# Maxima of the first six heads from a small float32 projection, batch 1's projection beside the first slots, layer change reordered

## The reference

```python
mod = jax.nn.silu(c) @ w_adaln + b_adaln
sh_msa, sc_msa, g_msa, sh_mlp, sc_mlp, g_mlp = jnp.split(mod, 6, axis=-1)
h = _modulate(_ln(x), sh_msa, sc_msa)
qkv = (h @ w_qkv + b_qkv).reshape(B, N, 3, nh, hd).transpose(2, 0, 3, 1, 4)   # 16 heads of 9
q, k, v = (qkv[0], qkv[1], qkv[2])
attn = jax.nn.softmax(jnp.einsum('bhqd,bhkd->bhqk', q, k) * hd ** (-0.5), axis=-1)
o = jnp.einsum('bhqk,bhkd->bhqd', attn, v).transpose(0, 2, 1, 3).reshape(B, N, C)
x = x + g_msa[:, None, :] * (o @ w_proj + b_proj)
xf = _modulate(_ln(x), sh_mlp, sc_mlp).reshape(-1, C)
topk_logits, topk_idx = jax.lax.top_k(xf @ w_gate, TOP_K)
gates = jax.nn.softmax(topk_logits, axis=-1)
cw = jnp.sum(jax.nn.one_hot(topk_idx, NUM_EXPERTS) * gates[..., None], axis=1)
hmid = jax.nn.gelu(jnp.einsum('tc,ech->eth', xf, w1) + b1[:, None, :], approximate=True)
eo = jnp.einsum('eth,ehc->etc', hmid, w2) + b2[:, None, :]
return x + g_mlp[:, None, :] * jnp.einsum('te,etc->tc', cw, eo).reshape(B, N, C)
# layer 1: the same attention, then x + gate * (gelu(h @ w_fc1 + b_fc1) @ w_fc2 + b_fc2)
```

## Time and profile before

| | us |
|---|---|
| median of 3 runs | 441.26 (441.07 to 442.12) |
| the profiled execution | 441.05 |
| its span, first to last instruction | 439.2 |
| PE busy | 392.8 (89%) |
| DVE busy | 299.6 (68%) |
| ACT busy | 216.9 (49%) |
| POOL busy | 83.4 (19%) |
| mean granted clock | 0.945 |

### The profile page before, as it was taken

How to read it: one execution, slowest core, us unless ns; L and a number is a source line. 1 busy time by engine, 2 the same in 40 slices (tenths; PEclk the granted TensorE clock), 3 DMA queues, 4 the chain that set the end, 5 groups by cost and what they waited for, 6 DMA issues and landing times.

```text
span 439.2 us, 5895 instructions
## 1 busy us (share of the span) xinstructions
PE 392.8 (89%) x1938; PEld 168.1 (38%) x1938; DVE 299.6 (68%) x838; ACT 216.9 (49%) x428; POOL 83.4 (19%) x137
## 2 busy tenths in 40 slices
PE   0996699989999897999999979978989999998896
PEld 0232122323334232585856625612333333322464
DVE  7755796878887934454376526798875888961643
ACT  1245015867776784504242331056764877586420
POOL 6997999200011000000000000000000110000000
PEclk9999555999999999999999999989996999999999
DMA  6065453369200000000000243000134100000001
GB/s 182 12 99 147 149 164 95 109 188 245 73 2 2 3 0 1 0 1 1 0 1 0 82 128 115 3 0 0 61 87 147 34 3 0 3 1 1 0 0 55
DMA packets 19657, 24.12 MB, mean 55 GB/s; under 512 B 5404, under 2 KB 15904, under 8 KB 19304
## 3 DMA queue, kind: packets, MB, share of 16 engines
q1 hardware_dynamic: 14360, 21.37, 16.4%
q0 software_dynamic: 3808, 1.73, 2.4%
q10 hardware_dynamic: 1460, 0.66, 0.5%
...
...
## 4 chain that ended last, share of the span: by engine, by line
PE 68%; DVE 15%; DMA 7%; ACT 4%; SPq 3%; issue 2%; DVEq 0%; ACTq 0%
PE bank L1258 13%; PE bank L1136 12%; PE bank L1273 11%; PE bank L1285 9%; PE bank L1236 8%; DVE nmax L946 8%; PE bank L1183 3%; ACT prob L1086 2%; PE bank L1303 2%; PE bank L1239 2%; DMA Qs<-qk_parts 2%; DMA qk_parts<-prob 2%; SPq L479 2%; DMA w<-in_L_cond_b_adaln_dram 2%; PE bank L1153 1%
## 5 line engine op out<-in xcount | busy, mean ns | idle before, releaser
L946 DVE TENSOR_REDUCE nmax<-bank 128x1 f32<-128x512 f32 x256 | 165.4, 682 | 35.7 <-PE bank L1273 34.6
L1086 ACT ACTIVATE prob<-bank 128x512 f32<-128x512 f32 x256 | 135.6, 602 | 46.5 <-PE bank L1285 46.0
L1273 PE MATMUL bank<-Ks,Qs 81*128 81x512 bf16 x256 | 105.1, 423 | 18.1 <-DMA Qs<-qk_parts 11.5
L1285 PE MATMUL bank<-Qs,Ks 83*128 83x512 bf16 x256 | 98.7, 398 | 6.5 <-ACT prob L1086 4.2
L1136 PE MATMUL bank<-prob,Va 128*32 128x512 f32 x512 | 71.7, 633 | 0.2
L587 POOL DMA_DIRECT2D Qs<-mT x24 | 13.6, 566 | 296.5 <-ACT mT L1093 251.8
L1273 PEld LDWEIGHTS bank<-Ks,Qs 81*128 81x128 bf16 x256 | 25.5, 102 | 90.9 <-DVE nmax L946 47.6
L1258 PE MATMUL bank<-w,big 128*128 128x144 f32 (+1 forms) x320 | 52.5, 305 | 0.2
L1075 ACT ACTIVATE big<-bank 128x512 f32<-128x512 f32 (+1 forms) x46 | 27.0, 597 | 49.6 <-PE bank L1239 49.6
L1258 PEld LDWEIGHTS bank<-w,big 128*128 128x128 f32 (+1 forms) x320 | 42.6, 188 | 10.6 <-DVE y L912 2.6
L1285 PEld LDWEIGHTS bank<-Qs,Ks 83*128 83x128 bf16 x256 | 25.3, 101 | 38.6 <-ACT prob L1086 17.0
...
## 6 DMA issues: line engine op xcount, KB each, us to landing
...
```

Source lines behind the costliest of these rows:

```text
L946: V.tensor_reduce(nmax[:, half, odd * NT + k:odd * NT + k + 1], bank[:, :], AX.X, ALU.max, negate=True).then_inc(s_free, 1)
L1086: A.activation(probs[:, k % 2, j, :], bank[:, :], ACT.Exp, scale=SCALE).then_inc(t_free, 1)
L1273: M.matmul(bank[:, :], Qs[b][0:MROW, h_, k4 * P:(k4 + 1) * P], Ks[b][0:MROW, h_, :], start=True, stop=True).then_inc(s_full, 1)
L1285: M.matmul(bank[:, :], Ks[b][0:SROWS, h0 + k4, k * P:(k + 1) * P], Qs[b][0:SROWS, h0 + k4, :], start=True, stop=True).then_inc(t_full, 1)
```

## The change

1. **Early maxima.** DVE also copies the columns of w_qkv of heads 0 to 3 and 4 to 7 into `wearly` and `wearly_stk`, each head's 9 columns at a multiple of 32. A stage `early` projects them (two float32 and two bf16 matmuls), ACT copies q and k to oT or hTb, and `emax` forms each 128 queries' scores of a head with a float32 matmul over 9 rows, in one of four row groups of the array. DVE takes the maxima of heads 0 to 5 of batch 0 from these; the six `max` stages go, the slots find units 0 to 5 done and go on with unit 6. Two stages `mturn` turn the first two pairs.
2. **Batch 1 of layer 0.** Its `turn` and two `ada` stages stand between the `emax` stages, and its `qkv` is spread over the places after slots (0,0) to (0,3). Its splits go to `beside`, and three steps are taken per tile (one before in layer 0, two in layer 1). Its pieces are read back later, the `late` loads start at the eighth slot.
3. **Transfers of maxima.** ACT issues those of the first 12 pairs, POOL the rest, SP none.
4. **Layer change.** layer 1's `turn` stands before the last chunk of `fc1`, and its `qkv` right after, ahead of both `fc2` stages; the bias sums have a stage `ybias`.
5. **Layer 1.** `turn` of batch 1 and the four parts of its `qkv` stand one slot earlier, its pieces one or two slots earlier.

```diff
     s = [("ada", 0, 0), ("ln", 0, 0), ("ada", 0, 1), ("ada", 0, 2), ("turn", 0, 0, "a"), ("ada", 1, 0),
-         ("ln", 0, 1), ("qkv", 0, 0, 0, QKV), ("ada", 1, 1), ("ada", 1, 2), ("turn", 0, 1, "a"), ("qkv", 0, 1, 0, QKV)]
-    s += [("max", 0, u) for u in range(UNIT_LEAD)]
+         ("ln", 0, 1), ("qkv", 0, 0, 0, 3), ("early", 0), ("qkv", 0, 0, 3, QKV), ("emax", 0, 0), ("early", 1),
+         ("emax", 0, 1), ("turn", 0, 1, "a"), ("emax", 0, 2), ("ada", 1, 1), ("emax", 0, 3), ("mturn", 0), ("mturn", 1)]
+    s += [("emax", 1, 0), ("ada", 1, 2)] + [("emax", 1, k) for k in range(1, NT)]
...
+            after[0, 0] = [("qkv", l, 1, 0, 1)]
+            after[0, 1] = [("qkv", l, 1, 1, 2)]
+            after[0, 2] = [("qkv", l, 1, 2, 3)]
+            after[0, 3] = [("qkv", l, 1, 3, QKV)]
         else:
-            after[0, 3] = [("turn", l, 1, "a")]
-            after[1, 0] = [("qkv", l, 1, 0, 1)]
-            after[1, 1] = [("qkv", l, 1, 1, 2)]
-            after[1, 2] = [("qkv", l, 1, 2, 3)]
-            after[1, 3] = [("qkv", l, 1, 3, QKV)]
+            after[0, 2] = [("turn", l, 1, "a")]
+            after[0, 3] = [("qkv", l, 1, 0, 1)]
+            after[1, 0] = [("qkv", l, 1, 1, 2)]
+            after[1, 1] = [("qkv", l, 1, 2, 3)]
+            after[1, 2] = [("qkv", l, 1, 3, QKV)]
...
-            s += [("ln", 1, 0), ("fc1", 1, 0, 0, CHH), ("turn", 1, 0, "a"), ("fc2", 1, 0, 0, 0, NT),
-                  ("qkv", 1, 0, 0, QKV), ("fc2", 1, 0, 1, 0, NT), ("fc1", 1, 1, 0, 5), ("max", B, 0),
+            s += [("ln", 1, 0), ("fc1", 1, 0, 0, CHH - 1), ("turn", 1, 0, "a"), ("ybias", 1), ("fc1", 1, 0, CHH - 1, CHH),
+                  ("qkv", 1, 0, 0, QKV), ("fc2", 1, 0, 0, 0, NT), ("fc2", 1, 0, 1, 0, NT), ("fc1", 1, 1, 0, 5), ("max", B, 0),
...
-PIECES_AT = (((0, 1), (0, 3), (1, 1), (1, 3)), ((2, 0), (2, 1), (2, 3), (3, 1)))
+PIECES_AT = (((1, 1), (1, 3), (2, 1), (2, 3)), ((1, 3), (2, 0), (2, 2), (3, 0)))
+EARLY = 6
+LATE_FROM = 7
...
+M_ACT = 12
...
-                if pair is not None and 2 * pair < NH:
-
-                    n, h = 2 * pair // NH, 2 * pair % NH
-                    sp.wait_ge(t_free, T_AT[i + 1])
-                    sp.dma_start(Qs[n % B][MROW:SROWS, h:h + 2, :], mT[:, pair % 2, :]).then_inc(m_in[pair % 4], 16)
...
+                elif kind == "emax":
+                    _, group, k = stage
+                    for h in early_heads(group):
+                        bank = take(s_at + h - G * group)
+                        V.tensor_reduce(nmax[:, h // 2 % 2, h % 2 * NT + k:h % 2 * NT + k + 1], bank[:, :], AX.X,
+                                        ALU.max, negate=True).then_inc(s_free, 1)
...
                             advance()
-                            if stage[1] and u < B * NH // 2:
+                            if u < B * NH // 2:
+                                advance()
                                 advance()
...
+                    if pair < M_ACT:
+                        n, h = 2 * pair // NH, 2 * pair % NH
+                        act.wait_ge(t_free, T_AT[i + 1])
+                        act.dma_start(Qs[n][MROW:SROWS, h:h + 2, :], mT[:, pair % 2, :]).then_inc(m_in[pair % 4], 16)
...
+                elif kind == "emax":
+                    _, group, k = stage
+                    pe.wait_ge(t_free, T_AT[WHERE[("early", group)] + 1])
+                    qk = qk_early[group]
+                    for h in early_heads(group):
+                        j = h - G * group
+                        rows = slice(P // G * j, P // G * j + HD)
+                        M.matmul(fill_s(s_at + j)[:, :], qk[rows, 0, k * P:(k + 1) * P], qk[rows, 1, :],
+                                 start=True, stop=True).then_inc(s_full, 1)
```

More of the change, by code:

```diff
@@ L147, in turns_pair @@
 def turns_pair(stage):
+    if stage[0] == "mturn":
+        return stage[1]
     if stage[0] not in ("max", "slot") or tiles_of(stage)[1] < NT:
@@ L166, in finishes, with early_heads @@
     return None, None
+def early_heads(group):
+    return range(G * group, min(G * (group + 1), EARLY))
 def banks_used(stage):
@@ L177, in banks_used @@
         t = stage[4] - stage[3]
+    elif kind == "early":
+        t = 2
+    elif kind == "emax":
+        s = len(early_heads(stage[1]))
     elif kind == "proj":
@@ L328, in build @@
         oN = [sb(f"oN{b}", [P, NT, C]) for b in range(B)]
[L329 removed]
+        hTb = sb("hTb", [P, B, N])
+        hT = {"a": [sb("hTa", [P, N])] * B, "b": [hTb[:, b, :] for b in range(B)]}
         hS = {"a": [sb("hSa", [ROWS, N], BF16)] * B, "b": [sb(f"hSb{b}", [ROWS, N], BF16) for b in range(B)]}
@@ L580, in _ @@
                 pair = turns_pair(stage)
-                if pair is not None and 2 * pair >= NH:
+                if pair is not None and pair >= M_ACT:
                     n, h = 2 * pair // NH, 2 * pair % NH
@@ L892, in _ @@
                         heads_innermost(1)
+                elif kind == "ybias":
+                    b = stage[1]
+                    finish()
+                    dve.wait_ge(cw_ready, b + 1)
+                    dve.wait_ge(ld_w[0], 16 * LATE0)
+                    for e in range(E):
+                        for k in range(NT):
+                            if e == 0:
+                                ins = V.tensor_scalar(y[:, k, :], b2bc[:, 0, :], cw[b][:, k, 0:1], None, ALU.mult)
+                            else:
+                                ins = V.scalar_tensor_tensor(y[:, k, :], b2bc[:, e, :], cw[b][:, k, e:e + 1],
+                                                             y[:, k, :], ALU.mult, ALU.add)
+                        link(ins)
                 elif kind == "fc2":
                     _, b, half, e2, lo, hi = stage
[L895 to L907 removed]
                     e = E2 * half + e2
@@ L1055, in _ @@
                                      ACT.Copy).then_inc(t_free, 1)
+                elif kind == "early":
+                    for w in range(2):
+                        bank = take(t_at + w)
+                        A.activation(qk_early[stage[1]][:, w, :], bank[:, :], ACT.Copy).then_inc(t_free, 1)
                 elif kind == "gate":
@@ L1090, in _ @@
                         at, count = m_landed(pair - 2)
-                        act.wait_ge((m_in if 2 * (pair - 2) < NH else m_pool)[at], count)
+                        act.wait_ge((m_in if pair - 2 < M_ACT else m_pool)[at], count)
                     bank = take(T_AT[i + 1] - 1)
@@ L1195, in _ @@
                         ins.then_inc(t_full, 1)
+                elif kind == "early":
+                    pe.wait_ge(early_ready, 1)
+                    pe.wait_ge(t_free, turned_at(WHERE[("qkv", 0, 0, 0, 3)]))
+                    for w in range(2):
+                        bank = fill_t(t_at + w)
+                        M.matmul(bank[:, :], wearly[:, stage[1], w, :], hT["a"][0][:, :], start=True, stop=False)
+                        M.matmul(bank[:, :], wearly_stk[:, stage[1], w, :], hS["a"][0][:, :], start=False, stop=True)\
+                            .then_inc(t_full, 1)
+                elif kind == "emax":
+                    _, group, k = stage
[6 more added lines that the diff above has]
+                                 start=True, stop=True).then_inc(s_full, 1)
                 elif kind == "proj":
@@ L1282, in _ @@
                             at, count = m_landed(pair)
-                            pe.wait_ge((m_in if 2 * pair < NH else m_pool)[at], count)
+                            pe.wait_ge((m_in if pair < M_ACT else m_pool)[at], count)
                         bank = fill_t(t_at + k4)
```

44 lines of the change are left out of this document (23 added, 21 removed).

## The result

| | us | ratio to before (95%) |
|---|---|---|
| before, median | 441.16 | |
| after, median of four | 445.85 | 1.0121 [1.0062, 1.018] |
| after once more, median of six | 446.55 (442.78 to 450.5) | 1.0102 [1.0052, 1.0153] |

The forecast was 439.1, so the sign was wrong; the time lies at the upper end of the range and beside rival B's (about 445). Single executions of one kernel scatter here, mostly by 4 to 9 us, so sizes are taken from the ratios, and places from profiles. A ratio compares executions in the faster of two states only, while the medians in us take in all, so that the two can differ by some tenths of a per cent, and more where a kernel scatters most.

The account below looks back on a forecast made before the run. It took DVE's maxima at the start, half clock on PE and waits for pieces at the layer change and in layer 1 as the bounds. Terms -1.5 + 8.4 + 0 - 3.9 - 5.2 = -2.2 us gave 439.1 us, range 437 to 441.5.

Parts of the forecast that it names:

- rival B: Start: the clock falls in the first groups of early maxima, before batch 1's transposes near 42 us; about 445 us, chance 0.25.
- Term 1: Start, up to unit 6's first maximum: early maxima avoid the wait for pieces; -4.8 + 3.3 = -1.5 us, bounds -4.8 and +5.5.
- 290 to 292: Trace stretch in the kernel before: DVE pacing, PE busy 0.61 of 2 us, half clock right behind; evidence against the clock staying up.
- Term 2: Slots (0,0) to (0,3): batch 1's projection and split move there, 25.3 us for 16.9; +8.4 us, bounds +3 and +10.
- the rule alone: Split steps beside POOL: a full wait for each of six two-input DVE steps would cost 7.6 us instead of 2.5.
- Rival A: Start: the clock stays up throughout, slots (0,0) to (0,3) take 22.6 us; sum -8.2, 433.1 us, chance 0.22.
- Term 3: Transfers of maxima issued from ACT: a late SP issue goes, ACT's exponentials wait somewhat; 0 us, bounds -1.1 and +1.3.
- Term 4: Layer change: earlier projection removes the 2.71 us wait for a piece and half clock behind it; -3.9 us, bounds -2.5 and -4.3.
- Term 5: Layer 1: batch 1's parts one slot earlier remove a 2.56 us wait and half clock; -5.2 us, bounds 0 and -5.4.
- rival D: Layer 1: its gain does not come because the piece still lands after PE wants it; up to +5, 444 us, chance 0.09.
- The likeliest case: Whole kernel: the forecast itself, 439.1 us, range 437 to 441.5, with the clock falling at about 50; chance 0.40.
- Rival C: Early score matmuls: the row groups run in turn, 24.5 us at full clock or 46 at half; 449 to 465 us, chance 0.04.

Follow-up runs that it names:

- k32: The changed kernel with the early score matmuls over all 32 rows of their row group instead of 9, the added rows zeros: 444.16 us, 1.0107 of before.
- l_slots: l_mact with part 2 alone added, batch 1's projection and split beside slots (0,0) to (0,3): 440.63 us, 1.0009 of before.
- l_mact: l_both with part 3 added, ACT issuing the transfers of the first 12 pairs and SP none: 431.87 us, 0.9838 of before.
- l_both: The kernel before with parts 4 and 5 alone, the new layer change and layer 1: 432.32 us, 0.9808 of before.
- l_change: The kernel before with part 4 alone, the new layer change: 433.33 us, 0.9806 of before.
- start_only: The changed kernel with the old layer change and old layer 1, so parts 1 to 3 alone: 452.09 us, 1.0274 of before.

## Why the prediction was wrong, point by point

**Term 1, the step that failed.** It took a fall of the clock at about 50; it came at 40.7, 0.3 us into the transposes of batch 1 and ahead of the 42 us from which rival B was to decide, and at 35.2 in the changed kernel's other profile. The row weighed against it, 290 to 292, pointed the right way, though PE was busy for 1.2 to 2.0 of each 2 us ahead of this fall, not for 0.6. DVE's own work was as forecast, 15.6 us of maxima and 2.0 of pairs against 14.6 and 2.3, and the start a microsecond earlier (33.27). But it stood idle for 17.0 us instead of 10.6: 2.7 for the small projection, as forecast, then 2.6 for the transposes (1.3), 3.4 and 2.8 for the two `ada` and the set behind each (0.9 and 0.5), 2.4 for the pairs (1.2), and 3.2 for the fourth tiles and the last sets (1.0). The term was +4.6, inside rival B's +2 to +5.5 (in the other profile +10.4, outside them). Beside the moment of the fall, its price was missed: the sum let each dry time grow by 0.9 at half clock, and they grew by 1.2 to 2.5. A dry time holds PE's work ahead of the set and the set's first result, and at half clock both took twice as long. k32, with a fall at 50.6, shows the start that had been forecast: unit 6 at 62.23, for 61.8.

**Term 2.** Near in sum, wrong in its parts. With unit 6 at 61.6, l_slots took 25.2 us for the forecast's 25.3, which is partly luck, and its ratio less l_mact's is +7.5 us for +8.4. POOL's 2.5 on the six steps with two inputs was right (2.3 there; the prediction's estimate by the rule alone, 7.6, was too much), but the 1.7 on the casts had no term, nor had the second half clock from 80.3. The rest was too high: with POOL held back the slots took 18.5, for 22.8. And rival B's +9 to +10 moved the wrong way: with unit 6 at 67.9 the slots took 21.5 us, and at 73.7 they took 19.6, since more of them lay behind POOL's end. Terms 1 and 2 aren't independent. Rival A's 22.6 us at full clock, beside POOL, stays untested: no profile has these slots with the projection and full clock throughout (k32's 25.5 has half clock to 67.6 and from 81.3).

**Term 3.** 0 was forecast; l_mact less l_both is +1.3 us by ratio, with intervals that overlap, and the changed kernel's stretch behind unit 10 is +0.9. An issue takes ACT 0.62 us ahead of the next exponentials (SP's took 0.71). The term is within its bounds and not told from 0.

**Term 4.** The wait and the half clock went, as worked out; l_change has no window under 1.00 between 240 and 264. In l_change's profile the layer change is 4.7 us shorter (forecast 3.9), in l_both's and the changed kernel's 2.7 and 2.4. The last isn't part 4's for certain: start_only, with the old order, has 124.1 us there, 2.1 less than before. By ratio l_change is 8.5 us faster, by medians 7.6. The other 3 to 4 are not explained: its profile has 1.9 of them ahead of unit 10, where its instructions are before's.

**Term 5.** This is rival D's size, not its cause: the piece came in time, but the slots ahead took the time back. The step "costs nothing while DVE sets the pace" was wrong: where DVE sets the pace, more steps in fewer slots make those slots longer. Net -1.6 at best, for -5.2.

**The sum.** Term 1 is 6.1 us over, terms 3 to 5 about 3.6, term 2 in the changed kernel 3.8 under. The likeliest case's chance of 0.40 was too high against rival B's 0.25, since the trace's nearest row spoke for B. Rival C fell: three row groups take 1.14 us, as the column groups did. The Trainium skill's 3.07 for four row tiles ("TensorE: Matmul & The Clock Gate", Part 3) is not tested by a set of three and one; three in 1.14 us, for 1.12 of one alone, don't speak against it.
